# Second edge stage of a graph network: maps written with edges on the partitions, the weighting of values on VectorE, maxima transposed earlier, selections by ScalarE as absolute difference and positive part

## What is computed

```python
ms = src_s[edge_src] + dst_s[edge_dst]            # 64 numbers an edge
mv = src_v[edge_src] + dst_v[edge_dst]            # 32 vectors of 3
w1, w2, w3, w4, w5 = split(h @ rw3 + roff)        # 224 weights an edge, h from an earlier stage
ds = concat(w1 * ms, w4 * dot(mv, Y1))            # 96
dv = concat(w2 * ms * Y1, w3 * mv, w5 * cross(mv, Y1))    # 128 vectors
ls, lv = eq_lin(ds, dv, lin_ws, lin_bs, lin_wv)   # the maps: 128 numbers, 32 vectors
a = einsum('ehk,hk->eh', smooth_leaky(alpha), alpha_dot)  # 8 heads; alpha is the first half of ls
a = exp(a - segment_max(a, edge_dst)[edge_dst])
a = a / segment_sum(a, edge_dst)[edge_dst]
ns = segment_sum(vs * a, edge_dst); nv = segment_sum(vv * a, edge_dst)
```

## Time and profile before

| what | us |
|---|---|
| median of 3 runs (lowest, highest) | 9799.34 (9798.74, 9811.15) |
| the profiled execution | 9813.87 |
| its span, from the first instruction to the last | 9812.0 |
| the window that the arithmetic below uses, 386 steps of the second edge stage | 3640 (from 5400 to 9040) |
| busy over the whole span: TensorE, VectorE, ScalarE, GpSimd | 8373.1, 7735.9, 4874.4, 7372.6 |

### The profile page before, as it was taken

One profiled execution on the slowest core, in us unless ns is written; L12 is line 12 of the kernel. 1 busy time (PEld: TensorE's weight loads), 2 busy tenths in 40 slices (PEclk: granted clock), 3 DMA queues, 4 the chain that ended last, 5 costly groups with the idle time before them and its releaser, 6 DMA issues. The chain is left out here.

```text
span 9812.0 us, 193495 instructions
## 1 busy us (share of the span) xinstructions
PE 8373.1 (85%) x35878; PEld 5079.2 (52%) x35878; DVE 7735.9 (79%) x14864; ACT 4874.4 (50%) x9073; POOL 7372.6 (75%) x4571
## 2 busy tenths in 40 slices
PE   0788888888888869999985999999999999998588
PEld 0444444444444422222222777777777777777233
DVE  3177777777777768888886999999999999998465
ACT  0176666666666631121121555555555555555355
POOL 4378888888888878778774888888888888886331
PEclk9599999999999989999997999999999999999799
DMA  5578888888888877778773666666666666665222
GB/s 208 180 161 167 167 168 166 167 167 167 167 167 167 167 213 275 267 271 282 264 270 109 136 137 144 137 143 137 144 138 144 138 142 137 144 137 122 59 70 52
DMA packets 1235170, 1618.04 MB, mean 165 GB/s; under 512 B 222610, under 2 KB 1010589, under 8 KB 1178973
## 3 DMA queue, kind: packets, MB, share of 16 engines
q1 hardware_dynamic: 758950, 1273.86, 40.0%
q0 software_dynamic: 475584, 338.58, 27.1%
HBM read 1533.79 MB, written 444.07 MB: 202 GB/s over the span
## 5 line engine op out<-in xcount | busy, mean ns | idle before, releaser
L1952 POOL DMA_INDIRECT e_m<-TS,e_at x1568 | 2631.8, 1678 | 583.7 <-issue 461.4
L442 POOL DMA_INDIRECT sums<-e_total,e_place x1568 | 2506.9, 1599 | 565.9 <-DMA sums<-e_total,e_place 314.5
L579 PE MATMUL ps<-e_win,e_pick 128*128 128x448 f32 x3136 | 1325.8, 568 | 165.0 <-DVE e_u L476 97.0
L579 PEld LDWEIGHTS ps<-e_win,e_pick 128*128 128x128 f32 x3136 | 612.5, 201 | 921.6 <-issue 864.1
L2275 ACT ACTIVATE e_dT<-ps 128x512 f32<-128x512 f32 x1176 | 660.0, 596 | 495.5 <-PE ps L2149 340.1
L2275 ACT ACTIVATE e_oT<-ps 128x512 f32<-128x512 f32 x784 | 468.9, 598 | 615.1 <-PE ps L2177 373.2
L742 DVE SCALAR_TENSOR_TENSOR r_y<-ps,w_rb,r_rstd 128x512 f32<-128x512 f32 x394 | 295.6, 750 | 579.9 <-issue 533.2
L1096 POOL TENSOR_TENSOR n_zv<-n_zv,n_ast 128x1536 f32<-128x1536 f32 x200 | 703.6, 3518 | 36.6 <-DMA n_zv<-in_x_groups 22.5
L1936 POOL TENSOR_TENSOR e_val<-e_val 128x640 f32<-128x640 f32 x392 | 670.9, 1712 | 61.9 <-ACT e_val L2252 61.9
L2018 DVE TENSOR_TENSOR e_q<-e_row,dstI 128x512 f32<-128x512 int32 x392 | 704.2, 1796 | 13.3 <-PE ps L2163 13.3
L711 PE MATMUL ps<-r_sq,w_avg 128*128 128x512 f32 x788 | 458.1, 666 | 277.4 <-issue 277.4
(11 more groups left out here) (448 smaller groups left out, 19299.8 us busy)
## 6 DMA issues: line engine op xcount, KB each, us to landing
e_win<-T SPq DMA_DIRECT2D x1568, 168.0 KB
n_z<-in_x_groups SPq DMA_DIRECT2D x400, 512.0 KB
n_zv<-in_x_groups SPq DMA_DIRECT2D x800, 192.0 KB
TOT<-e_tot SPq DMA_DIRECT2D x392, 352.0 KB, 2.6
e_row<-in_src_rows SPq DMA_DIRECT2D x98, 1024.0 KB
e_local<-LR SPq DMA_DIRECT2D x196, 512.0 KB
e_row<-in_dst_rows SPq DMA_DIRECT2D x98, 1024.0 KB
e_win<-TD SPq DMA_DIRECT2D x1568, 60.0 KB
```

Of the source, the lines that this page charges most:

```text
L442: pool.indirect_dma_start(sums[c], bass.IndirectOffsetOnAxis(ap=place[:, r % 4, c:c + 1], axis=0), total[:, r % 4, c, 0:MSG0], None, compu ...
L579: pe.matmul(g[:, c, :], pick[:, p, R * c:R * c + R], win[:, s, c, :], start=True, stop=True).then_inc(spread, 1)
L1952: pool.indirect_dma_start(m_[:, r % 4, c, :], None, TS, bass.IndirectOffsetOnAxis(ap=at[:, gp, col:col + 1], axis=0), compute_op=ALU.add). ...
```

## The change

The maps take the transposed edges `dT` as the operand that is held and stream the weights, four products of 128 streamed columns for the scalars and eight for the vectors, so that the result has edges on the partitions at once; `oT`, two of the five `keep` copies and both `turn_back` steps go. Their results lie in two PSUM banks with one copy each, `scalar_out4` and `vector_out4`, so that the maps of step i wait for VectorE's results(i-1): the scalar map for its first operation (`silued`), the vector maps for its last reading (`freed`). ScalarE's results(i) move into its own step i.

`weighted` moves from GpSimd, eight steps late, to the front of VectorE's body, six steps late. `selections` moves from VectorE to ScalarE, between the copies keep 1 and keep 2, as two operations: the absolute difference, then the positive part of one minus it. `tops_down` moves to a place ahead of the wait for `d_ready` and the transpositions of the scan step. `weigh_up` moves from the end of ScalarE's scan step to the next step, behind its two `keep_far`. VectorE's results make alpha's product first.

```diff
...
-        oT = sb("e1_oT", [128, 2, GT * R])
...
+        minus, one = sb("e1_minus", [128, 1]), sb("e1_one", [128, 1])
...
-        out4 = ps[0:R, 4:6, :].rearrange("r b (c x) -> r (b c) x", c=2)
+        scalar_out4 = ps[0:R, 4, :].rearrange("r (c x) -> r c x", c=GT)
+        vector_out4 = ps[0:R, 5, :].rearrange("r (c x) -> r c x", c=GT)
...
         def bank(i, j):
-            return 2 + (7 * i.r + j) % 2
+            return 2 + (5 * i.r + j) % 2
...
-                        if not i.before(8):
-                            weighted(i, 8)
...
-                    dve.tensor_scalar(pick[:, p, :], local[:, gp, GT * R * s:GT * R * s + GT * R], iota[:, 0:1], None,
-                                      ALU.is_equal).then_inc(picked, 1)
...
                     dve.wait_ge(outs, i.n(2, 2))
+                    s3 = silu[:, p].rearrange("r c (h x) -> r c h x", h=HEADS)
+                    dve.scalar_tensor_tensor(out=silu[:, p], in0=silu[:, p], scalar=1.5, in1=alpha4, op0=ALU.add, op1=ALU.mult
+                                             ).then_inc(silued, 1)
+                    gate(dve, k)
+                    dve.wait_ge(mapped, i.n(2, 2))
...
+                    gate(dve, k)
+                    dve.wait_ge(silued, i.n(2, 1))
+                    dve.tensor_tensor(silu[:, p], silu[:, p], bc(W["ad"][0:R, :], GT, 1), ALU.mult).then_inc(silued, 1)
                     gate(dve, k)
                     dve.wait_ge(by_y, i.n(1, 1))
                     dve.tensor_tensor(values(i)[:, :, :, 9:SEG], vectors4[:, :, :, 0:12],
                                       turn_by_y[:].rearrange("r (c h) x -> r c h x", c=GT), ALU.add).then_inc(freed, 1)
                     gate(dve, k)
-                    dve.wait_ge(silued, i.n(2, 1))
-                    dve.tensor_tensor(silu[:, p], silu[:, p], bc(W["ad"][0:R, :], GT, 1), ALU.mult).then_inc(silued, 1)
-                    gate(dve, k)
                     dve.wait_ge(silued, i.n(2, 2))
                     dve.tensor_reduce(values(i)[:, :, :, 0], s3, AX.X, ALU.add).then_inc(logit, 1)
...
+                def weighted(i):
+
+                    j = i.r - 6
+                    slot, gp = j % STEPS, j % STEPS // 4
+                    gate(dve, k)
+                    dve.wait_ge(exped, i.uses(2, j // 4 + 1))
+                    u = val[:, gp, 4 * (slot % 4):4 * (slot % 4) + 4].rearrange("r c (h x) -> r (c h) x", x=SEG)
+                    dve.tensor_tensor(u[:, :, 1:SEG], u[:, :, 1:SEG], bc(u[:, :, 0], SEG - 1, 2), ALU.mult
+                                      ).then_inc(u_ready, 1)
...
+                        if not i.before(6):
+                            weighted(i)
                         if more:
                             sums(after)
                         if r % 4 == 1 and not i.before(5):
                             scans(i)
-                        if i.plus(4).within():
-                            selections(i.plus(4))
                         if not i.before(1):
                             results(i.plus(-1))
...
                 def map_scalars(i):
                     gate(pe, k)
-                    pe.wait_ge(kept, i.n(5, 2))
...
+                    pe.wait_ge(kept, i.n(3, 1))
+                    if not i.before(1):
+                        gate(pe, k)
+                        pe.wait_ge(outs, i.n(2))
+                        gate(pe, k)
+                        pe.wait_ge(silued, i.n(2, -1))
+                    for c in range(GT):
+                        last = pe.matmul(scalar_out4[:, c], dT[:, 0, R * c:R * c + R],
+                                         W["la"][:].rearrange("u a h x -> u (a h x)"), start=True, stop=True)
+                    last.then_inc(mapped, 1)
 
                 def map_vectors(i):
                     gate(pe, k)
-                    pe.wait_ge(kept, i.n(5, 3))
...
+                    pe.wait_ge(kept, i.n(3, 3))
+                    if not i.before(1):
                         gate(pe, k)
                         pe.wait_ge(freed, i.n(1))
                     for c in range(GT):
-                        last = pe.transpose(out4[:, c, 128 * j:128 * j + 128], oT[:, j, R * c:R * c + R], I[:])
+                        pe.matmul(vector_out4[:, c], dT[:, 1, R * c:R * c + R], W["lb"][:].rearrange("u h x -> u (h x)"),
+                                  start=True, stop=False)
+                        last = pe.matmul(vector_out4[:, c], dT[:, 2, R * c:R * c + R],
+                                         W["lc"][:].rearrange("u h x -> u (h x)"), start=False, stop=True)
                     last.then_inc(mapped, 1)
...
                         if i.plus(3).within():
-                            spread_out(i.plus(3), 0, far2(i, 0), (far_kept, 5) if i.before(1) else (kept, i.n(5, -1)))
-                        if not i.before(1):
-                            turn_back(i.plus(-1), 0)
-                        if i.plus(3).within():
-                            spread_out(i.plus(3), 1, far2(i, 1), (far_kept, 6) if i.before(1) else (kept, i.n(5)))
-                        if not i.before(1):
-                            turn_back(i.plus(-1), 1)
+                            spread_out(i.plus(3), 0, far2(i, 0), (far_kept, 5) if i.before(1) else (kept, i.n(3, -1)))
+                            spread_out(i.plus(3), 1, far2(i, 1), (far_kept, 6) if i.before(1) else (kept, i.n(3)))
                         if not (isinstance(t, int) and t == PASSES - 1 and r == STEPS - 1):
                             weights(after)
+                        if r % 4 == 1 and not i.before(5):
+                            tops_down(i)
                         gate(pe, k)
                         pe.wait_ge(d_ready, i.n(1, 1))
                         turn(i, 0)
                         turn(i, 1)
+                        map_scalars(i)
+                        turn(i, 2)
                         if not i.before(6):
                             totals(i, 0)
-                        turn(i, 2)
-                        if r % 4 == 1 and not i.before(5):
-                            tops_down(i)
-                        map_scalars(i)
+                        map_vectors(i)
                         if not i.before(6):
                             totals(i, 1)
-                        map_vectors(i)
                         if r % 4 == 0 and not i.before(4):
                             logits_up(i)
...
+                def selections(i):
+
+                    p, s, gp = i.r % 2, i.r % 4, i.r // 4
+                    gate(act, k)
+                    act.wait_ge(local_here[gp], i.uses(16, 16))
+                    if not i.before(2):
+                        gate(act, k)
+                        act.wait_ge(spread, i.n(2, 2, 2))
+                    act.activation(pick[:, p, :], local[:, gp, GT * R * s:GT * R * s + GT * R], ACT.Abs, bias=minus[:, 0:1]
+                                   ).then_inc(distant, 1)
+                    gate(act, k)
+                    act.wait_ge(distant, i.n(1, 1))
+                    act.activation(pick[:, p, :], pick[:, p, :], ACT.Relu, bias=one[:, 0:1], scale=-1.0).then_inc(picked, 1)
...
-                    act.wait_ge(mapped, i.n(2, 2))
...
@@ -2304,26 +2304,28 @@
                         if i.plus(3).within():
                             keep_far(i.plus(3), 0, far2(i, 0))
                             keep_far(i.plus(3), 1, far2(i, 1))
-                        if not i.before(1):
-                            results(i.plus(-1))
+                        if r % 4 == 2 and not i.before(6):
+                            weigh_up(i.plus(-1))
                         keep(i, 0)
                         keep(i, 1)
+                        if i.plus(4).within():
+                            selections(i.plus(4))
+                        keep(i, 2)
+                        results(i)
                         if not i.before(6):
                             keep_totals(i, 0)
-                        keep(i, 2)
-                        keep(i, 3)
-                        if not i.before(6):
                             keep_totals(i, 1)
-                        if r % 4 == 1 and not i.before(5):
-                            weigh_up(i)
-                        keep(i, 4)
...
```

More of the change, by code:

```diff
@@ L1953, in body @@
                                 ap=at[:, gp, col:col + 1], axis=0), compute_op=ALU.add).then_inc(rows_here[r % 4], 16)
-                        if not i.before(8):
-                            weighted(i, 8)
                 passes(pool, body)
-                for r in range(8):
-                    weighted(At(PASSES, r), 8)
             @block.vector
             def _(dve):
-                def selections(i):
-                    p, s, gp = i.r % 2, i.r % 4, i.r // 4
-                    gate(dve, k)
-                    dve.wait_ge(local_here[gp], i.uses(16, 16))
-                    if not i.before(2):
-                        gate(dve, k)
-                        dve.wait_ge(spread, i.n(2, 2, 2))
```

(35 more changed lines are left out.)

26 lines of the change are left out of this document (10 added, 16 removed).

## The result

| | median us | runs, us | profiled span |
|---|---|---|---|
| before | 9799.04 | 9794.77 to 9811.15 | 9812.0 |
| after | 10009.17 | 9965.83 to 10016.37 | 10012.1 |

The changed kernel takes 1.0203 of the time of the one before (95% interval 1.0173 to 1.0234): 2.0% slower, some 210 us. The forecast was 9803 with a range of 9690 to 9950, so the time lies above the range.

A forecast was written before the change was run, and what follows sets the result against it. VectorE was taken to bound the kernel before. After the change, eight steps of 75.1 us (9.39 a step) plus 0.04 for scatter gave 9.43 again; +4 us for epilogue and rounding up of waits made 9803, range 9690 to 9950.

The forecast's parts named there:

- TensorE's sum, 7.66: TensorE's work in one step after the change, without waits: weights, turns, maps, totals and spreads, 7.66 us.
- Short passes at 0.11: TensorE's maps in 24 short passes: 0.11 us each, scalar map 0.87 and vector maps 1.74, as before.
- The scalar map at T + 1.38: TensorE starts it 1.38 us after the step's first transposition (T), a wait of 0.51 for ScalarE's copy.
- The vector maps at T + 3.66: TensorE starts them 3.66 us after the step's first transposition, a wait of 0.40 for ScalarE's copy keep 2.
- the rival's mark of 2.95: Selections delay TensorE once ScalarE's copy keep 2 starts later than about 2.95 us after the first transposition.
- TensorE's period without other waits: TensorE's step from its work plus 0.91 us of waits for ScalarE's copies: 8.57 us.
- The loop through the maxima: After a scan step VectorE's `weighted` waits for ScalarE's exponential, queued behind TensorE's scan step: 3.8 us idle a group.
- the loop's turn: VectorE's wait at each turn of the program loop, once in eight steps: 1.5 us added to every second group.
- The selections hold TensorE: ScalarE's selection pair delays copies TensorE needs, 0.35 us a step; about 9940 us; chance 0.19.
- load-bound: Loading held operands paces TensorE's 24 short passes at 0.14 us, 0.7 more a step; 10080 us; chance 0.04.
- e_q stays slow: GpSimd's gathers hold VectorE's e_q and `weighted`, + 0.85 us a step; 10130 us; chance 0.04.
- The loop is covered: VectorE finds the exponential ready, so its work of 8.45 us sets the step; 9415 us; chance 0.09.

The follow-up runs named there:

- e1: Changed kernel with SyncE storing the totals of step i - 7 instead of i - 6; 9804.11 us, ratio 0.9978 to the kernel before.
- e4: e3 with the selections back on VectorE as one comparison and without ScalarE's pair; 9730.99 us, ratio 0.9907 to the kernel before.
- e3: Changed kernel with stores one step later and `weighted` behind the next step's sums on VectorE; 9594.99 us, ratio 0.9772 to the kernel before.
- e5: e3 with first totals between second and third turn, scalar map behind all turns, ScalarE's selections behind the copies TensorE needs; 9457.17 us, ratio 0.9615.
- e7: e1 with `weighted` back on GpSimd, behind the gathers and eight steps late; 9805.15 us, ratio 0.9975 to the kernel before.

## Why the prediction was wrong

**The step that failed** is a term that the working put at nothing without a reason: TensorE's waits for SyncE's transfers. The working moved the second totals behind the vector maps and counted them in TensorE's sum, 7.66, but did not follow their result any further. SyncE's store waits for their copy, in order, ahead of the next windows and e_h, and TensorE came to wait 6.2 us in eight steps for these. The last sentence of the prediction warned of SyncE's windows and gave no price. The trace before had most of what was needed for one: by the working's own times the second totals start at T + 3.66 + 1.74 = 5.40, 2.66 later than before; e_h had 5.3 to 7.4 us from issue to use, less 2.66 makes 2.6 to 4.7, and its transfer, for which the trace after shows 2.5 us and in some steps about 5, would use it up in some steps. That was a rival with a price, and e1 shows that it is the whole loss: without it the ratio is 0.9978, not 1.0203.

**The sum behind it stands, by the size of its result.** e1 is the changed kernel without SyncE's part, at 9.39 a step where the working has 9.39. In time it is 18 us below the kernel before of its own group of runs (9804.11 against 9821.85), where the forecast was 4 above: that 9804.11 is so near to 9803 is chance, as the kernel before took 23 us more in that group. Most of the 22 us between is the allowance of 0.04 a step for scatter, 16 us, which was not needed. Its terms:
- e_q 0.68: measured 0.681. `weighted` 0.81: 0.820. VectorE's work fell as summed.
- Short passes at 0.11: 16 of the vector maps take 1.88 from the first start to the start of what follows, 0.117 each. The rival's 0.14 did not come; the term of 1.74 was 0.14 too small.
- The scalar map at T + 1.38: measured 1.29 in an undisturbed step of e1. The vector maps at T + 3.66: measured 3.62. The timeline of e1 shows both waits, with the pair of selections that lies between:

```profile
7110.34 1.04 PE L2140 MATMUL ps<-ident,e_d 128*128 128x128 f32 x8
...
7111.63 1.16 PE L2167 MATMUL ps<-w_la,e_dT 128*128 128x128 f32 x8 [0.25 <-ACT e_dT L2275]
...
7111.95 0.72 ACT L2255 ACTIVATE e_pick<-e_local,e_minus 128x512 f32<-128x512 bf16 x1
...
7112.71 0.72 ACT L2259 ACTIVATE e_pick<-e_pick,e_one 128x512 f32<-128x512 f32 x1
...
7113.34 0.58 ACT L2275 ACTIVATE e_dT<-ps 128x512 f32<-128x512 f32 x1
...
7113.97 0.49 PE L2178 MATMUL ps<-w_lb,e_dT 128*128 128x128 f32 x2 [0.17 <-issue]
```

- The selections: 0.62 each was mis-sized, 0.72 measured. Keep 2 starts 3.00 behind T in the fence above, past the rival's mark of 2.95, but the vector maps follow it by 0.63 and not 0.75, and so start 0.04 earlier than worked out. The rival's 0.35 a step did not come. TensorE's period without other waits is 8.69 against 8.57, and the 0.12 lies behind that start, for the most part in the vector maps.
- The loop through the maxima: in the step after a scan step the scalar map is at T + 3.45 and 3.54 where it is at 1.29 in an undisturbed one, so it waits 2.2 more, against 2.16 in the working.

**Two errors in it cancel.** VectorE's idle time at the group's head is 4.5 in e1, not 3.8, and the loop's turn, for which I added 1.5 to every second group, doesn't show: the two groups of a turn take 37.4 and 37.7 in e1, where the working has 36.8 and 38.3. In the timeline of e1 `weighted` follows e_q without a gap across the turn. In e4, where VectorE is near its end, the turn shows again, at 1.0. Why it hides in e1 was not tested. That 9.39 came out to the last digit is thus luck; its mechanism, three engines closed in a ring by the exponential, is shown by e3, where opening the ring is worth 209 us.

**The rivals.** "The selections hold TensorE" (9940), "load-bound" (10080) and "e_q stays slow" (10130) all lay nearer to the time that came than the forecast, each for a reason that did not come. "The loop is covered" at 9415 needs the ring opened, which the changed kernel doesn't do; e3 opens it and is bound by TensorE at 9595, and e5 comes to 9457. "e_q stays slow" fell with e_q at 0.681, "load-bound" with the maps at 0.117. The condition that I had set for each could be read off the profile; none of the four had a transfer in it, and neither the range nor the chance of slower had a case for one.

## What to carry to other kernels

When an operation is moved, follow its result to the last reader, a store included, and then list what is queued behind that reader on its engine: here a store that nobody waits for cost 2%, since the next inputs stood behind it. On the queue that prefetches, issue a store a step later than its data: that was worth 2.2% in the changed kernel and 0.4% in the one before. When an engine is relieved and nothing gets faster, look for the operation at the head of its body that waits for a far result, and put work that needs nothing ahead of it.

## What the hardware showed that I had not expected

- GpSimd's product holds nearly whichever of VectorE's operations with two SBUF inputs meets it: e_cr from 0.55 to 2.20 in 159 cases of e7, the product with w_ad from 0.41 to 1.90 in 76. One with a single tensor from SBUF was held as well: the scans' multiplication of e_mask took 2.57 in the 8 cases that met it, 0.23 elsewhere. Moving the weighting back made another victim, not the same one.
- Two ScalarE operations of 128x512 within SBUF, with a bias from SBUF, take 0.72 each, where a copy of that shape takes 0.62.
- A turn of the loop costs SyncE more than VectorE: in the turn shown it takes 5.0 us from its last store to its first window, 3.2 of it from the branch on, where other steps have 1.6 to 2.2 in all; VectorE's turn costs 1.5. The kernel before has 4.5 there and e1 4.9. In the changed kernel that comes on top of the store's wait, and step 0 is the longest, 12.72 on average.
- TensorE's start on e_h, where it waits for it, comes 2.5 to 2.8 us after the issue, and about 5 us after it where a load of e_local was issued just ahead and one of e_row just behind.
